# A Perceiver layer on one core: the softmax denominators of its local attention, from key tiles added up on GpSimd

## The chip, the cores and the metric

The kernel runs on one core of a Trainium2 chip. The metric is the device time of one launch in microseconds, as the median of several runs. The engines are TensorE (PE; its weight loads are PEld), VectorE (DVE), ScalarE (ACT), GpSimd (POOL) and SyncE (SP), which here starts the DMAs.

## The reference

A latent x of 512 tokens with 512 channels passes three blocks: cross-attention to 8192 context tokens with an MLP behind it, causal local self-attention, and a gated feed-forward block with FP4 rounding. The change is in the second:

```python
qkv = layernorm(x) @ Wqkv                      # 16 heads of 32 channels
q, k = rope(q), rope(k)
dist = idx[None, :] - idx[:, None]
allowed = (dist <= 0) & (dist >= -255)         # a window of 256 keys
scores = where(allowed, q @ k.T / sqrt(32), -inf)
x = x + (softmax(scores) @ v) @ Wout
```

All of it is in float32; the kernel splits values into float16 halves where it multiplies them in float16.

## The kernel before

The program has four stages, one after the other: projections of the context, cross-attention (the longest), the local attention (names that begin with `local_`), and the feed-forward block (`ffn_`). Each engine has its own instruction list, written out by Python loops, and engines wait for each other by semaphores.

The local stage first makes q, k and v. VectorE, GpSimd and ScalarE apply the rotary embedding there: GpSimd multiplies by the cosines (`t_cos`, L1771), VectorE by the sines (L1859), and VectorE adds both (L1862). The DMA then stacks the float16 halves in `kq_stack`, and later turns the feed-forward weights with transposing DMAs.

Then follow 16 groups, one for each query tile t (128 tokens) and each g of four heads. Query tile 0 sees one key tile, tile 1 two, tiles 2 and 3 three each. The loop on TensorE is a pipeline over rounds n (L2103). In round n it makes:

- `scores_for_maxima(n, u)`: scores of group n with queries on partitions, so that VectorE (`maxima`, L1880) can take row maxima; unit u holds four, two or one heads. The banks of `pre_ps` alternate;
- `row(n - 1)` (L2048): these maxima turned into one row; ScalarE (`set_row`, L1807) copies it into `kq_stack`, where the next product subtracts it;
- `turned_scores(n - 2, i)` (L2062, with the mask L2066): scores with keys on partitions, for key tile i. ScalarE (`exps`, L1815) writes their exponentials to `prT`, a ring of 8 tiles;
- `values(n - 3, step)` (L2083): for each key tile four products with v, and four with a matrix of ones which sum the exponentials over keys, all in float32. The first nk steps are values, the next nk are ones, two steps for each u;
- `back(n - 5)` (L2098): the output projection of a group.

VectorE, in its round n, does `maxima(n, 0)`, then `normalise(n - 4)` (a reciprocal of the denominators L1887, a product L1890), then the other maxima. Behind these stand either `add` (L1895, L1900; rounds 9, 13, 17) or up to three pieces of `first_tile` (L1912 to L1951), which prepares the first tile of the feed-forward block out of the latent: in round 11 L1921 / L1924, L1925 / L1927, L1928, in round 12 L1924, L1925 / L1927, L1928 / L1924, L1925, in round 14 L1927, L1928 / L1930 / L1933, in round 15 L1936, L1937 / L1939, L1940 / L1942, in round 16 L1945 / L1947 / L1949. ScalarE makes the float16 high half of the output (`high_out`, L1820) and GpSimd the low half `o_low` (L1776), its only work in these rounds.

Of the kernel before, what the change touches and what calls it, by code (L numbers as in the profile page):

```python
# [22 lines left out]
ALU = mybir.AluOpType  # L23
# [7 lines left out]
P = 128  # L31
T = 512
D = 512
# [6 lines left out]
HD = D // H  # L40
G = 4
HG = H // G
# [20 lines left out]
TILE_RING = 8  # L63
# [19 lines left out]
class Chain:  # L83
# [14 lines left out]
    def wait(self):  # L98
        self.eng.wait_ge(self.sem, self.n + self.moving)
# [35 lines left out]
def perceiver(nc, a, out):  # L135

    with ExitStack() as whole:
# [1514 lines left out]
        with ExitStack() as st:  # L1652
# [12 lines left out]
            kq_stack = sb("kq_stack", [P, 2, H, T], F16)  # L1665
            v = sb("v_local", [P, TT, D])
            prT = sb("prT", [P, TILE_RING, D])
            top = sb("top", [P, 2, HG], F16)
            inv = sb("inv", [P, 2, P])
            o_norm = sb("o_norm", [P, 2, P])  # L1670
# [10 lines left out]
            turned_out = sem("turned_out_l")  # L1681
            qk_ready = sem("qk_ready")
            qk_out = sem("qk_out")
            rot_ready = sem("rot_ready")
            cos_done = sem("cos_done")
            roped = sem("roped")
            r_high = sem("r_high")
            r_low = sem("r_low")
# [29 lines left out]
            pre_upto = [sum(pre_units[:n + 1]) for n in range(NG)]  # L1718
            tiles_upto = [sum(seen[t][1] for t, _ in groups[:n + 1]) for n in range(NG)]


            pre_turns = []
            for n in range(NG + 1):
# [39 lines left out]
            @block.gpsimd  # L1763
            def _(pool):
                pool.wait_ge(const_in, 64)
                nc.gpsimd.tensor_copy(maskb[:], mask[:]).then_inc(consts, 1)
                nc.gpsimd.tensor_copy(identb[:], ident[:]).then_inc(consts, 1)
                for m in range(2 * G):
                    pool.wait_ge(qk_out, m + 1)
                    wait(pool, roped, m - 1)  # L1770
                    nc.gpsimd.tensor_tensor(t_cos[:, m % 2], qk[:, m % 2], cos[:], ALU.mult).then_inc(cos_done, 1)  # L1771
                for n, (t, g) in enumerate(groups):
                    pool.wait_ge(o_scaled, n + 1)
                    pool.wait_ge(o_high, n + 1)
                    tokens = slice(t * P, (t + 1) * P)
                    nc.gpsimd.tensor_tensor(oT[:, 1, g, tokens], o_norm[:, n % 2], oT[:, 0, g, tokens],  # L1776
                                            ALU.subtract).then_inc(o_low, 1)

            @block.scalar
            def _(act):  # L1780
                layer_norm_scalar(act, var_ready, sd_ready, 2)
                for t in range(TT):
                    act.wait_ge(turned, t + 1)
                    nc.scalar.activation(xnT[:, 0, :, t * P:(t + 1) * P], by_chunk(t), ACT.Copy).then_inc(turned_high, 1)

                def high(m):

                    act.wait_ge(roped, m + 1)
                    nc.scalar.activation(r_hi[:, m // G, m % G], rotated[:, m % 2], ACT.Copy,
                                         scale=(1.0, SCALE)[m // G]).then_inc(r_high, 1)  # L1790

                for m in range(2 * G):
                    if m >= 2:
                        high(m - 2)
                    act.wait_ge(qk_ready, m + 1)
                    wait(act, roped, m - 1)
                    nc.scalar.activation(qk[:, m % 2], s_ps[:, 0, m % 2], ACT.Copy, scale=1.0 / WSCALE).then_inc(qk_out, 1)
                high(2 * G - 2)
                high(2 * G - 1)
                for t in range(TT):  # L1800
                    act.wait_ge(v_ready, t + 1)
                    nc.scalar.activation(v[:, t], t_ps[:, t % 2], ACT.Copy, scale=1.0 / WSCALE).then_inc(v_read, 1)

                def set_row(n):
                    t, g = groups[n]
                    act.wait_ge(row_ready, n + 1)
                    nc.scalar.activation(kq_stack[KROWS:KROWS + 1, 1, g * HG:(g + 1) * HG, t * P:(t + 1) * P],  # L1807
                                         pre_ps[KROWS:KROWS + 1, turn_of[("row", n, 0)] % 2].rearrange("p (j q) -> p j q", j=HG),
                                         ACT.Copy).then_inc(row_set, 1)

                def exps(n, i):
                    c = tiles_upto[n] - seen[groups[n][0]][1] + i
                    act.wait_ge(s_ready, c + 1)
                    wait(act, p_read, c + 1 - TILE_RING)
                    nc.scalar.activation(prT[:, c % TILE_RING], score_ps[:, c % 2], ACT.Exp).then_inc(p_ready, 1)  # L1815

                def high_out(n):
                    t, g = groups[n]
                    act.wait_ge(o_scaled, n + 1)
                    nc.scalar.activation(oT[:, 0, g, t * P:(t + 1) * P], o_norm[:, n % 2], ACT.Copy).then_inc(o_high, 1)  # L1820

                for n in range(NG + 4):
                    tiles = seen[groups[n - 2][0]][1] if 2 <= n < NG + 2 else 0
                    if tiles:
                        exps(n - 2, 0)
                    if 1 <= n <= NG:
                        set_row(n - 1)
                    for i in range(1, tiles):
                        exps(n - 2, i)
                    if n >= 4:  # L1830
                        high_out(n - 4)
                    if n == NG + 3:
                        act.wait_ge(first_turned, 1)
                        nc.scalar.activation(first_T[:, 0], pre_ps[:, 0].rearrange("p (k c) -> p k c", c=P),
                                             ACT.Copy).then_inc(first_high, 1)

            @block.vector
            def _(dve):
# [15 lines left out]

                for m in range(2 * G):

                    dve.wait_ge(rot_ready, m + 1)
                    wait(dve, roped, m - 1)
                    chain.link(nc.vector.tensor_tensor(t_sin[:, m % 2], s_ps[:, 1, m % 2], sin[:], ALU.mult))  # L1859
                    dve.wait_ge(cos_done, m + 1)  # L1860
                    wait(dve, r_low, m - 1)
                    nc.vector.tensor_tensor(rotated[:, m % 2], t_cos[:, m % 2], t_sin[:, m % 2], ALU.add).then_inc(roped, 1)  # L1862
                    if m >= 1:
                        low(m - 1)
# [19 lines left out]

                def normalise(n):
                    dve.wait_ge(p_read, tiles_upto[n])
                    nc.vector.reciprocal(inv[:, n % 2], od_ps[:, n % 2, P:2 * P]).then_inc(inv_ready, 1)  # L1887
                    dve.wait_ge(inv_ready, n + 1)
                    wait(dve, o_low, n - 1)
                    nc.vector.tensor_tensor(o_norm[:, n % 2], od_ps[:, n % 2, 0:P], inv[:, n % 2],  # L1890
                                            ALU.mult).then_inc(o_scaled, 1)
# [91 lines left out]
            def _(pe):  # L1983
# [9 lines left out]
                def rotate(m):  # L1993
                    pe.wait_ge(qk_out, m + 1)
                    wait(pe, roped, m - 1)
                    nc.tensor.matmul(s_ps[:, 1, m % 2], rot[:], qk[:, m % 2], start=True, stop=True).then_inc(rot_ready, 1)

                for m in range(2 * G):
                    wait(pe, qk_out, m - 1)
# [67 lines left out]
                                                    start=False, stop=True)  # L2067
                    last.then_inc(s_ready, 1)

                def values(n, step):  # L2070


                    t, g = groups[n]
                    k0, nk = seen[t]
                    at, i = divmod(step, nk)
                    c = tiles_upto[n] - nk + i
                    if at == 0:
                        pe.wait_ge(p_ready, c + 1)
                    if step == 0:
                        wait(pe, o_scaled, n - 1)  # L2080
                    for j in range(HG):
                        head = g * HG + j
                        last = nc.tensor.matmul(od_ps[j * HD:(j + 1) * HD, n % 2, at * P:(at + 1) * P],  # L2083
                                                ones[:] if at else v[:, k0 + i, head * HD:(head + 1) * HD],
                                                prT[:, c % TILE_RING, j * P:(j + 1) * P], start=i == 0, stop=i == nk - 1)
                    if at:
                        last.then_inc(p_read, 1)

                def back(n):

# [12 lines left out]
                for n in range(NG + 5):  # L2103
# [3 lines left out]
                    for u in range(max(units, scored, weighted, 1)):  # L2107
                        if u < units:
                            scores_for_maxima(n, u)
                        if u < scored:  # L2110
                            turned_scores(n - 2, u)
                        if u < weighted:
                            values(n - 3, 2 * u)
                            values(n - 3, 2 * u + 1)
                        if u == 0 and 1 <= n <= NG:
                            row(n - 1)
                    if n >= 5:
                        back(n - 5)
                    if n == NG + 3:
# [352 lines left out]
```

## Time and profile before

| | |
|---|---|
| median of 3 runs | 1332.82 us (1330.89 to 1335.74) |
| the profiled execution | 1333.27 us |
| its span, first to last instruction | 1331.4 us |
| granted TensorE clock, mean | 0.995 of full speed |
| the 16 groups of local attention | about 1156 to 1229 us of the span |
| TensorE, VectorE, ScalarE, GpSimd busy in 1157.0 to 1229.2 us (72.2 us) | 67.0, 56.3, 36.4, 7.2 us |

A time in a row counts from the start of the span. "Busy" of TensorE includes the pipelined ends of its products, so the distance between two starts says more than the length of one. A bracket at the end of a row is the idle time of the engine just before it and the operation that ended it.

### The profile page before, as it was taken

To read this page: it belongs to the slowest core of one execution; us is meant where nothing else is said; L and a number is where in the kernel's file an instruction comes from. 1 tells how busy PE (TensorE), PEld (TensorE's weight loads), DVE (VectorE), ACT (ScalarE), POOL (GpSimd) and SP (SyncE) were. 2 spreads that over 40 slices of the span, in tenths; PEclk is the share of its full clock that TensorE was granted. 3 is DMA by queue.
4 is the path that set the end of the run, shared out by engine and by line. 5 is a ranking of instruction groups with operands and counts; after the bars stand their busy time and mean duration, and the time that the engine had idled before them with its cause. 6 is when DMAs were issued, how large, how long until landed. Compare 5 with 4: busy or idle time off the path is not lost. (4 is left out here: it accounts for less than half of the span.)

```text
span 1331.4 us, 39304 instructions
## 1 busy us (share of the span) xinstructions
PE 1292.7 (97%) x16386; PEld 673.5 (51%) x16386; DVE 1084.9 (81%) x1791; ACT 989.2 (74%) x2026; POOL 717.5 (54%) x340
## 2 busy tenths in 40 slices
PE   8999999998999999999999999999999999999998
PEld 5444444443455555555555555555554445576454
DVE  6678888886888988888888888888986665588885
ACT  5456654564999999999999999999999832354332
POOL 1322222124788988888898889889887001111121
PEclk9999999999999999999999999999999999999999
DMA  8687886775462122122212221221211040690000
GB/s 274 189 204 220 248 241 183 203 234 152 119 190 77 40 72 69 36 66 68 72 40 71 70 56 55 65 67 37 72 59 31 4 151 1 143 215 2 1 9 25
DMA packets 127799, 137.50 MB, mean 103 GB/s; under 512 B 44995, under 2 KB 108995, under 8 KB 125699
## 3 DMA queue, kind: packets, MB, share of 16 engines
q1 hardware_dynamic: 127622, 134.98, 36.1%
q8 instruction: 130, 2.13, 0.7%
q14 instruction: 47, 0.39, 0.1%
HBM read 75.70 MB, written 44.17 MB: 90 GB/s over the span
## 5 line engine op out<-in xcount | busy, mean ns | idle before, releaser
L1444 DVE TENSOR_REDUCE early<-attend_banks 128x1 f32<-128x512 f32 x952 | 590.0, 682 | 66.1 <-PE attend_banks L1144 64.7
L1602 POOL TENSOR_TENSOR early<-early,attend_prob 128x1152 f32<-128x1152 f32 x210 | 556.6, 2650 | 43.1 <-ACT attend_prob L1401 22.9
L1401 ACT ACTIVATE attend_prob<-attend_banks 128x512 f32<-128x512 f32 x1024 | 555.5, 600 | 20.8 <-PE attend_banks L1184 12.7
L1184 PE MATMUL attend_banks<-early,k_first 97*32 97x512 f16 x2560 | 269.2, 383 | 5.6 <-PEq L303 4.0
L1144 PE MATMUL attend_banks<-k_first,early 96*32 96x512 f16 x2272 | 214.8, 383 | 0.6
L1184 PE MATMUL attend_banks<-early,attend_k_rest 97*32 97x512 f16 x1536 | 160.8, 380 | 1.1 <-ACT attend_prob L1401 0.9
L1357 ACT ACTIVATE attend_banks<-attend_banks,early 128x512 f32<-128x512 f32 x238 | 160.1, 673 | 0.0
L1144 PE MATMUL attend_banks<-attend_k_rest,early 96*32 96x512 f16 x1536 | 142.4, 379 | 0.0
L1197 PE MATMUL attend_banks<-attend_prob,wkv_area 128*32 128x512 f32 x1024 | 136.0, 592 | 0.0
L1197 PE MATMUL attend_banks<-attend_prob,attend_vh_odd 128*32 128x512 f32 x1024 | 135.2, 592 | 0.0
L1144 PEld LDWEIGHTS attend_banks<-k_first,early 96*32 96x32 f16 x2272 | 74.5, 96 | 100.3 <-DVE early L1444 74.5
L532 POOL TENSOR_TENSOR project_w_whole<-project_grid,project_qscale 128x704 f32<-128x704 f32 x24 | 34.8, 1452 | 165.7 <-DVE project_w_out L713 111.4
L1184 PEld LDWEIGHTS attend_banks<-early,k_first 97*32 97x32 f16 x2560 | 84.9, 96 | 51.7 <-ACT attend_prob L1401 35.9
L1208 PE MATMUL attend_banks<-attend_prob,ones 128*32 128x96 f32 x2208 | 96.0, 245 | 0.0
L590 ACT ACTIVATE project_v<-project_v_ps 128x512 f32<-128x512 f32 x64 | 38.0, 599 | 77.8 <-PE project_v_ps L868 77.8
L1208 PEld LDWEIGHTS attend_banks<-attend_prob,ones 128*32 128x32 f32 x2208 | 75.4, 110 | 35.4 <-issue 1.2
L1144 PEld LDWEIGHTS attend_banks<-attend_k_rest,early 96*32 96x32 f16 x1536 | 48.9, 95 | 66.4 <-DVE early L1444 50.3
L521 POOL TENSOR_TENSOR project_qn<-early,project_qinv 128x704 f32<-128x704 f32 x24 | 36.3, 1514 | 71.0 <-issue 42.1
L866 PE MATMUL project_v_ps<-project_w_hi,project_yT_hi 128*128 128x512 f16 x192 | 73.2, 381 | 0.7 <-ACT project_v L590 0.7
L849 PE MATMUL project_k_ps<-project_yT_hi,project_w_hi 128*128 128x512 f16 x192 | 72.5, 379 | 1.0 <-ACT project_yT_hi L556 1.0
L868 PE MATMUL project_v_ps<-project_w_hi,project_yT_lo 128*128 128x512 f16 x192 | 73.0, 380 | 0.0
L867 PE MATMUL project_v_ps<-project_w_lo,project_yT_hi 128*128 128x512 f16 x192 | 73.0, 380 | 0.0
(233 smaller groups left out, 1963.2 us busy)
## 6 DMA issues: line engine op xcount, KB each, us to landing
v_scratch<-project_v SPq DMA_DIRECT2D x16, 1024.0 KB, 8.3
early<-in_ctx_dram SPq DMA_DIRECT2D x16, 768.0 KB, 6.4
k_first<-k_scratch SPq DMA_DIRECT2D x36, 256.0 KB, 3.4
k_scratch<-project_k_hi SPq DMA_DIRECT2D x64, 128.0 KB, 2.9
k_scratch<-project_k_lo SPq DMA_DIRECT2D x64, 128.0 KB, 3.1
attend_vh_odd<-v_scratch SPq DMA_DIRECT2D x8, 1024.0 KB, 5.3
wkv_area<-v_scratch SPq DMA_DIRECT2D x7, 1024.0 KB, 5.1
attend_k_rest<-k_scratch SPq DMA_DIRECT2D x24, 256.0 KB, 3.4
```

The lines of the kernel that those rows point to most:

```text
L849: last = nc.tensor.matmul(k_ps[:, g % 2], (w_lo if p == 2 else w_hi)[:, 0, k, cols], (yT_lo if p == 1 else yT_hi)[:, u, k], start=(k, p) = ...
L866: nc.tensor.matmul(v_ps[:, t % 2], yT_hi[:, u, k, cols], w_hi[:, 1, k], start=k == 0, stop=False)
L867: nc.tensor.matmul(v_ps[:, t % 2], yT_hi[:, u, k, cols], w_lo[:, 1, k], start=False, stop=False)
L868: last = nc.tensor.matmul(v_ps[:, t % 2], yT_lo[:, u, k, cols], w_hi[:, 1, k], start=False, stop=k == CK - 1)
L1144: last = nc.tensor.matmul(pre_ps[c * HD:(c + 1) * HD, bank, :], q_stack[0:KROWS, h, queries], keys_at(s, part * BLK, (part + 1) * BLK)[0:K ...
L1184: last = nc.tensor.matmul(s_ps[c * HD:(c + 1) * HD, s_bank(h, n), :], key_rows[:, c * HD:(c + 1) * HD], q_stack[0:KROWS + 1, h, :], start= ...
L1197: last = nc.tensor.matmul(pv_ps[t * HD:(t + 1) * HD, :], vh[s][:, BT * q + t, :], prob[:, q % PSLOTS, t, :], start=q == 0, stop=q == QUADS ...
L1208: last = nc.tensor.matmul(den_ps[t * HD:(t + 1) * HD, 0:P - HD], ones[:], of_block(prob[:, q % PSLOTS, n, 0:ADDED], t), start=q == 0 and n ...
L1357: nc.scalar.activation(pre_ps[:, bank], pre_ps[:, bank], ACT.Exp, bias=tile_low[:, s, SUM_J, part:part + 1], accum_out=part_sum[:, s, part ...
L1401: nc.scalar.activation(prob[:, q % PSLOTS, t, :], s_ps[:, s_bank(h, BT * q + t)], ACT.Exp).then_inc(p_ready, 1)
L1444: nc.vector.tensor_reduce(tile_low[:, s, j, part:part + 1], pre_ps[:, bank], AX.X, ALU.max, negate=True).then_inc(pre_read, 1)
L1602: nc.gpsimd.tensor_tensor(sums, sums, prob[:, q % PSLOTS, 0:POOL_TILES, 0:ADDED], ALU.add).then_inc(pool_summed, 1)
```

## The change

The exponentials of a group's two or three key tiles are added on GpSimd into `tile_sum` (two buffers), and TensorE makes one set of four ones-products from the sum. This holds for the groups 4 to 14. The groups 0 to 3 have one tile, and the last group keeps its three sets. `values(n, i)` now makes only value products, one key tile for each u; the ones-products stand in `denominators(n)`, behind all units of the round and ahead of `back`. `rot_ready` is renamed `side_ready` and counts the denominators too; `cos_done` is renamed `pool_made` and counts the sums too. GpSimd issues the sums of group n before the low half of group n - 2. An exponential waits for the sum that reads its old tile.

```diff
+            tile_sum = sb("tile_sum", [P, 2, D])
...
+            def summed(n):
+                return seen[groups[n][0]][1] > 1 and n < NG - 1
+            def sums_until(n):
+                return 2 * G + sum(seen[groups[k][0]][1] - 1 for k in range(n + 1) if summed(k))
...
-                for n, (t, g) in enumerate(groups):
-                    pool.wait_ge(o_scaled, n + 1)
-                    pool.wait_ge(o_high, n + 1)
-                    tokens = slice(t * P, (t + 1) * P)
-                    nc.gpsimd.tensor_tensor(oT[:, 1, g, tokens], o_norm[:, n % 2], oT[:, 0, g, tokens],
-                                            ALU.subtract).then_inc(o_low, 1)
+                def sum_tiles(n):
+                    nk = seen[groups[n][0]][1]
+                    c0 = tiles_upto[n] - nk
+                    pool.wait_ge(p_ready, c0 + 2)
+                    pool.wait_ge(side_ready, 2 * G + n - 1)
+                    nc.gpsimd.tensor_tensor(tile_sum[:, n % 2], prT[:, c0 % TILE_RING], prT[:, (c0 + 1) % TILE_RING],
+                                            ALU.add).then_inc(pool_made, 1)
+                    if nk == 3:
+                        pool.wait_ge(p_ready, c0 + 3)
+                        pool.wait_ge(pool_made, sums_until(n) - 1)
+                        nc.gpsimd.tensor_tensor(tile_sum[:, n % 2], tile_sum[:, n % 2], prT[:, (c0 + 2) % TILE_RING],
+                                                ALU.add).then_inc(pool_made, 1)
+
+                for n in range(NG + 2):
+                    if n < NG and summed(n):
+                        sum_tiles(n)
+                    if n >= 2:
+                        t, g = groups[n - 2]
+                        pool.wait_ge(o_scaled, n - 1)
+                        pool.wait_ge(o_high, n - 1)
+                        tokens = slice(t * P, (t + 1) * P)
+                        nc.gpsimd.tensor_tensor(oT[:, 1, g, tokens], o_norm[:, n % 2], oT[:, 0, g, tokens],
+                                                ALU.subtract).then_inc(o_low, 1)
...
 def exps(n, i):
-                    wait(act, p_read, c + 1 - TILE_RING)
+                    if c >= TILE_RING:
+                        act.wait_ge(p_read, c + 1 - TILE_RING)
+                        before = next(k for k in range(NG) if tiles_upto[k] > c - TILE_RING)
+                        if summed(before):
+                            act.wait_ge(pool_made, sums_until(before))
+                        else:
+                            act.wait_ge(side_ready, 2 * G + before + 1)
...
 def normalise(n):
                     dve.wait_ge(p_read, tiles_upto[n])
+                    dve.wait_ge(side_ready, 2 * G + n + 1)
...
-                def values(n, step):
+                def values(n, i):
-                    at, i = divmod(step, nk)
-                    if at == 0:
-                        pe.wait_ge(p_ready, c + 1)
-                    if step == 0:
+                    pe.wait_ge(p_ready, c + 1)
+                    if i == 0:
                         wait(pe, o_scaled, n - 1)
                     for j in range(HG):
                         head = g * HG + j
-                        last = nc.tensor.matmul(od_ps[j * HD:(j + 1) * HD, n % 2, at * P:(at + 1) * P],
-                                                ones[:] if at else v[:, k0 + i, head * HD:(head + 1) * HD],
+                        last = nc.tensor.matmul(od_ps[j * HD:(j + 1) * HD, n % 2, 0:P], v[:, k0 + i, head * HD:(head + 1) * HD],
                                                 prT[:, c % TILE_RING, j * P:(j + 1) * P], start=i == 0, stop=i == nk - 1)
-                    if at:
-                        last.then_inc(p_read, 1)
+                    last.then_inc(p_read, 1)
+
+                def denominators(n):
+                    nk = seen[groups[n][0]][1]
+                    if summed(n):
+                        pe.wait_ge(pool_made, sums_until(n))
+                        tiles = [tile_sum[:, n % 2]]
+                    else:
+                        tiles = [prT[:, (tiles_upto[n] - nk + i) % TILE_RING] for i in range(nk)]
+                    for i, tile in enumerate(tiles):
+                        for j in range(HG):
+                            last = nc.tensor.matmul(od_ps[j * HD:(j + 1) * HD, n % 2, P:2 * P], ones[:],
+                                                    tile[:, j * P:(j + 1) * P], start=i == 0, stop=i == len(tiles) - 1)
+                    last.then_inc(side_ready, 1)
...
                         if u < weighted:
-                            values(n - 3, 2 * u)
-                            values(n - 3, 2 * u + 1)
+                            values(n - 3, u)
                         if u == 0 and 1 <= n <= NG:
                             row(n - 1)
+                    if weighted:
+                        denominators(n - 3)
                     if n >= 5:
                         back(n - 5)
```

## Rows read from the trace of the kernel before

**Rows 1.** The page: the span, and busy time, share and instructions of an engine.

```profile
span 1331.4 us, 39304 instructions
...
PE 1292.7 (97%) x16386; PEld 673.5 (51%) x16386; DVE 1084.9 (81%) x1791; ACT 989.2 (74%) x2026; POOL 717.5 (54%) x340
```

**Rows 2.** Groups by shape, PE, 1156 to 1229.3 us: busy, mean ns, idle before.

```profile
L2083 PE MATMUL local_t_ps<-local_prT,ones 128*32 128x128 f32 x288 | 12.3, 276 | 0.0
```

**Rows 3.** Timeline of PE, one round: start, length, operation, [idle before].

```profile
1199.23 0.22 PE L2066 MATMUL local_sl_ps<-local_identb,local_maskb 128*128 128x128 bf16 x1
1199.38 0.64 PE L2083 MATMUL local_t_ps<-local_prT,local_v_local 128*32 128x128 f32 x16
1199.86 0.39 PE L2048 MATMUL local_sl_ps<-identh,local_top 128*1 128x128 f16 x4
1200.34 0.34 PE L2034 MATMUL local_sl_ps<-local_kq_stack 96*128 96x384 f16 x1
...
1202.36 0.64 PE L2083 MATMUL local_t_ps<-local_prT,ones 128*32 128x128 f32 x16
1202.94 0.34 PE L2034 MATMUL local_sl_ps<-local_kq_stack 96*128 96x384 f16 x1
```

**Rows 4.** Timeline of PE: max(n,1) of rounds 11, 12, 14, 15.

```profile
1189.82 0.34 PE L2034 MATMUL local_sl_ps<-local_kq_stack 96*128 96x384 f16 x1 [0.44 <-DVE local_top L1880]
...
1195.00 0.34 PE L2034 MATMUL local_sl_ps<-local_kq_stack 96*128 96x384 f16 x1
...
1205.83 0.34 PE L2034 MATMUL local_sl_ps<-local_kq_stack 96*128 96x384 f16 x1 [0.25 <-DVE local_top L1880]
...
1211.69 0.34 PE L2034 MATMUL local_sl_ps<-local_kq_stack 96*128 96x384 f16 x1 [0.62 <-DVE local_top L1880]
```

**Rows 5.** Timeline of DVE, rounds 14 to 17.

```profile
1208.92 0.56 DVE L1880 TENSOR_REDUCE local_top<-local_sl_ps 128x1 f16<-128x384 f32 x1 [0.86 <-PE local_sl_ps L2039]
1209.39 0.14 DVE L1927 TENSOR_SCALAR r<-r 128x1 f32<-128x1 f32 x1
...
1215.26 0.17 DVE L1936 TENSOR_SCALAR late<-late 128x32 f32<-128x32 f32 x1
...
1220.47 0.96 DVE L1887 RECIPROCAL local_inv<-local_t_ps 128x128 f32<-128x128 f32 x1
```

**Rows 6.** Timeline of ACT, exponentials of rounds 14 and 16.

```profile
1206.54 0.60 ACT L1815 ACTIVATE local_prT<-local_sl_ps 128x512 f32<-128x512 f32 x1 [0.33 <-PE local_sl_ps L2062]
1207.96 0.60 ACT L1815 ACTIVATE local_prT<-local_sl_ps 128x512 f32<-128x512 f32 x1 [0.83 <-PE local_sl_ps L2066]
...
1217.31 0.60 ACT L1815 ACTIVATE local_prT<-local_sl_ps 128x512 f32<-128x512 f32 x1
```

**Rows 7.** Stretches: length, busy us of each engine.

```profile
1215.00:1225.00 10.00, 10.00 (x198) 6.89 (x197) 9.59 (x19) 4.88 (x10) 1.65 (x4) 1.00 0.01 3
```

**Rows 8.** One line: ns min/median/max.

```profile
L1771 POOL TENSOR_TENSOR turned_area<-turned_area,early x8: 1264/1268/1271, 1118.2 to 1141.5; 128x512 f32<-128x512 f32 x8
```

**Rows 9.** The same for DVE's addition of two SBUF operands.

```profile
L1862 DVE TENSOR_TENSOR turned_area<-turned_area x8: 691/904/906, 1121.8 to 1144.5; 128x512 f32<-128x512 f32 x8
```

**Rows 10.** Timeline of POOL and DVE, ropes of the local stage.

```profile
1124.23 1.27 POOL L1771 TENSOR_TENSOR turned_area<-turned_area,early 128x512 f32<-128x512 f32 x1 [2.18 <-ACT turned_area L1797]
...
1125.14 0.91 DVE L1862 TENSOR_TENSOR turned_area<-turned_area 128x512 f32<-128x512 f32 x1
```

**Rows 11.** Timeline of POOL and DVE, feed-forward stage.

```profile
1279.49 1.15 POOL L2231 TENSOR_TENSOR ffn_hqT<-ffn_whole_T,ffn_hqT 128x512 f16<-128x512 f32 x1 [6.46 <-ACT ffn_whole_T L2259]
1279.85 0.83 DVE L2300 TENSOR_SCALAR ffn_qscale_f<-ffn_amax_f 128x32 f32<-128x32 f32 x1
```

**Rows 12.** Timeline of DVE and POOL, round 16.

```profile
1218.91 0.69 DVE L1947 TENSOR_TENSOR late<-late 128x512 f32<-128x512 f32 x1
...
1219.11 0.78 POOL L1776 TENSOR_TENSOR late<-local_o_norm,late 128x128 f16<-128x128 f32 x1 [3.91 <-ACT late L1820]
```

**Rows 13.** Timeline of POOL, attention stage: two sums in a row.

```profile
487.54 2.65 POOL L1602 TENSOR_TENSOR early<-early,attend_prob 128x1152 f32<-128x1152 f32 x1 [0.24 <-ACT attend_prob L1401]
```

More of the change, by code:

```diff
@@ L1683, in perceiver @@
             qk_out = sem("qk_out")
-            rot_ready = sem("rot_ready")
-            cos_done = sem("cos_done")
+            side_ready = sem("side_ready")
+            pool_made = sem("pool_made")
             roped = sem("roped")
@@ L1770, in _ @@
                     wait(pool, roped, m - 1)
-                    nc.gpsimd.tensor_tensor(t_cos[:, m % 2], qk[:, m % 2], cos[:], ALU.mult).then_inc(cos_done, 1)
-                for n, (t, g) in enumerate(groups):
-                    pool.wait_ge(o_scaled, n + 1)
-                    pool.wait_ge(o_high, n + 1)
-                    tokens = slice(t * P, (t + 1) * P)
-                    nc.gpsimd.tensor_tensor(oT[:, 1, g, tokens], o_norm[:, n % 2], oT[:, 0, g, tokens],
-                                            ALU.subtract).then_inc(o_low, 1)
+                    nc.gpsimd.tensor_tensor(t_cos[:, m % 2], qk[:, m % 2], cos[:], ALU.mult).then_inc(pool_made, 1)
+                def sum_tiles(n):
[20 more added lines that the diff above has]
+                                                ALU.subtract).then_inc(o_low, 1)
             @block.scalar
@@ L1855, in _ @@
                 for m in range(2 * G):
-                    dve.wait_ge(rot_ready, m + 1)
+                    dve.wait_ge(side_ready, m + 1)
                     wait(dve, roped, m - 1)
                     chain.link(nc.vector.tensor_tensor(t_sin[:, m % 2], s_ps[:, 1, m % 2], sin[:], ALU.mult))
-                    dve.wait_ge(cos_done, m + 1)
+                    dve.wait_ge(pool_made, m + 1)
                     wait(dve, r_low, m - 1)
@@ L1995, in rotate @@
                     wait(pe, roped, m - 1)
-                    nc.tensor.matmul(s_ps[:, 1, m % 2], rot[:], qk[:, m % 2], start=True, stop=True).then_inc(rot_ready, 1)
+                    nc.tensor.matmul(s_ps[:, 1, m % 2], rot[:], qk[:, m % 2], start=True, stop=True).then_inc(side_ready, 1)
                 for m in range(2 * G):
```

## The prediction

> **What bounds the kernel now.** I read the page first: TensorE is busy for 97% of 1331.4 us [rows 1]. The groups by line between 1156 and 1229 us, the part of the local stage that the diff touches, come next: 288 records of ones-products, two to a product, so 144 products, 12.3 us busy, with no idle time before them [rows 2]. A mean of 276 ns is pipelined length, not cost; the cost is the pitch, and for that the timeline of one round is needed.
>
> A round n is one pass of the loop at L2103. I call max(n,u) the products of `scores_for_maxima(n, u)`, and S(n) the start of max(n,1), which waits until VectorE has reduced max(n,0), as they share a bank. S is 1189.82, 1195.00, 1200.34, 1205.83, 1211.69 for n = 11 to 15 [rows 3, 4], so the rounds from 11 to 14 last 5.18, 5.34, 5.49 and 5.86. In round 11 TensorE has no wait, in 13 and 14 it waits at the end for `local_top` (0.25, 0.62) [rows 4], and in 12 VectorE is nearly as late.
>
> A round has two halves. From max(n,1) to max(n,3), 1200.34 to 1202.94, TensorE alone sets the pace: 2.60 us [rows 3]. VectorE then idles 0.86 before the last reduction, which starts at S + 3.09, and goes on at S + 3.56 with the steps of `first_tile` [rows 5]. From max(n,3) to S(n+1) TensorE needs 5.18 - 2.60 = 2.58 (round 11), and VectorE needs 0.49 to be released, the reduction, the steps, the next reduction. So in rounds 12 to 14 both halves must be asked separately. After the last reduction (round 15) VectorE is the bound: 9.59 us busy in the 10 us from 1215 to 1225 (third busy figure of the row) [rows 7].
>
> **What is removed on TensorE.** 16 records from 1199.38 to 1199.86 are 0.48 us, 0.03 a record; a set of four products (one key tile) is 8 records, 0.24 us [rows 3]. Entering the f32 products costs 0.09 (1199.23 + the pitch of 0.06 = 1199.29, start 1199.38), leaving them for products with a full weight load costs 0.10 (16 records take 0.58 from 1202.36 to 1202.94) [rows 3]. Groups 4 to 14 are summed. In a round with three key tiles six sets become four: -0.48. The ones now stand by themselves ahead of `back`: one more entry and exit, +0.19. TensorE's round becomes 5.18 - 0.29 = 4.89. The half after max(n,1) loses two sets, -0.48; the half after max(n,3) gains 0.43 and loses the one value set that moves to u = 1, +0.19.
>
> **Where it arrives.** In rounds 3 and 4 the ones move behind `row`, whose result ScalarE turns into the wait of the next scores: about -0.2 each. In rounds 5 and 6 nothing waits and nothing is saved: +0.19 each. Rounds 7 to 9 (two key tiles): -0.24 + 0.19 each. Round 10: VectorE's steps end it, but its middle half is a set shorter, -0.24. Together -0.4. From round 11 on the middle half brings VectorE's last reduction 0.48 forward, which is worth 0.48 wherever VectorE ends the round, and 0.29 where TensorE does.
>
> **What is added on GpSimd.** Up to two additions of 128x512 f32 a round, 1.27 us each by the same shape and operation kind [rows 8]. ScalarE's exponential of tile 1 starts at S + 0.71 and ends at S + 1.31 [rows 4, 6]. That of tile 2, now at S + 2.13 [rows 4, 6], comes 0.24 sooner and ends at S + 2.49. With 0.1 for the release the first addition runs from S + 1.4 to S + 2.67. The second also waits for the first; the gap of such a pair is 0.24 [rows 13], so it runs from S + 2.91 to S + 4.18. Between 0.05 and 0.3 for that gap moves this end by 0.2. TensorE wants the sum at the end of the next round, S(n+1) + 2.4 or so: 3 us spare, no wait. Queued behind the second addition is `o_low` of the group two before, late by at most 1 us at S + 4.7. Its reader `back` stands in the next round, `normalise` in the one after: covered. `o_low` frees o_norm for a normalise two rounds off; covered. The wait of the exponentials on the sum of the tile eight back is for one that ended a round before: nothing, and without that cover it would stop ScalarE by the lateness. The added waits on VectorE (16) and ScalarE find their value there; their own cost is between 0 and 0.03 each (the pitch of VectorE's small steps leaves no more), I take 0. Denominators come later but VectorE's `normalise` stands behind max(n,0), behind them on TensorE: nothing.
>
> **What the additions meet.** This is the largest term. DVE's L1862, two SBUF operands, takes 691 ns with no GpSimd work beside it and 904 with it [rows 9]: at 1125.14 it found L1771 running until 1125.50 and ended at 1126.05, 0.55 after that [rows 10]. It was stopped until GpSimd was done. A `tensor_scalar` of 128x32, SBUF to SBUF, ended at 1280.68, 0.04 after GpSimd's 1280.64, and took 0.83 [rows 11], where my S(15) row of the same shape took 0.17 [rows 5]. It goes the other way too: a 128x128 `o_low`, issued at 1219.11 under L1947, took 0.78 [rows 12], of which 0.49 lay before L1947's end at 1219.60. The reductions, `normalise` and `add` have a PSUM operand or one SBUF operand; only steps of `first_tile` pay. With VectorE's 0.48 gain they now begin at S + 3.08, inside the second addition, which holds them until S + 4.18:
> - round 11: its second step (L1924, two operands) should end at 3.43, ends at 4.20: +0.77. Net -0.48 + 0.77 = +0.29.
> - round 12: the first step is L1924: +0.96, net +0.48.
> - round 13: `add` and bn_stats, not stopped: -0.48 (5.01, above TensorE's 4.89).
> - round 14: the second step, L1928: +0.77, net +0.29.
> - round 15: the first step L1936 (the shape of [rows 11]): 3.25 becomes 4.22, +0.97; less 0.48, +0.49.
> - round 16: exponential 1 of group 14 starts at S(15) + 5.62 [rows 4, 6], about 0.3 sooner after; group 14's additions run at 6.05 to 7.32 and 7.56 to 8.83. VectorE's L1947 comes at about 7.7, would end at 8.4, and ends 0.55 after 8.83: +0.99. VectorE has no room there [rows 5, 7], and `normalise(13)` (1220.47) and all behind it move.
>
> The Trainium skill ("SBUF — State Buffer", section "Who interferes with whom") says that a VectorE instruction with two SBUF inputs, or in a two-port mode, and a reading GpSimd instruction exclude each other, and that whichever issues second blocks fully. The trace agrees with the exclusion, but not to the last 0.14 us: a full 0.69 after 1125.50 would end L1862 at 1126.19, and it ended at 1126.05 [rows 10]. By the rule read so the sum would be 6 x 0.14 = 0.8 us higher than below.
>
> **Sum.** -0.4 + 0.29 + 0.48 - 0.48 + 0.29 + 0.49 + 0.99 = +1.7 us. The profiled execution took 1333.27 us, with 1.9 around its span; the median shown is 1332.82. On the median this gives 1334.5.
>
> **Rivals.**
> 1. The stops don't fall there (the additions start 1 us earlier or later than worked out, or VectorE's steps slip between them). Then only TensorE and VectorE count: -0.4, round 11 -0.29, round 12 -0.45 (TensorE's 4.89 bounds), 13, 14 and 15 -0.48 each: -2.6, or 1330.2. For it: two of the six hits are single steps of 0.15 us. Against: the window is 1.27 us wide and begins before the steps do.
> 2. Slower: the stops multiply. GpSimd's `o_low` follows at once and takes the operands again before VectorE's next step; 0.3 in rounds 11, 12 and 15 (0.9), full restarts (6 x 0.14), and the one-element steps of round 10 stopped as well (0.6; no row shows that shape beside GpSimd): 1.7 + 2.3 = +4.0, or 1336.8. It decides when GpSimd's next start beats VectorE's next issue, some 0.1 us apart by my times.
> 3. Slower: GpSimd's sums come late and TensorE waits at `denominators`. It needs 3 us of lateness; in round 17 only 0.3 is spare, but there VectorE is the bound. If every round of three tiles paid 1 us: +7, 1340.
>
> **How the numbers follow.** The forecast gets 0.62, rival 1 0.22, rival 2 0.11, rival 3 0.03, anything else 0.02. No case but the third leaves 0.3% (4.0 us, about what this kernel's measurement can tell) far behind. The forecast's own range is -0.5 (gaps of 0.05, one hit less) to +3 (two `o_low` stops): 1332.3 to 1335.8. With the bounds of the first two rivals, and both signs: 1330.0 to 1337.0. Faster by over 0.3% 0.04, slower 0.09 (half of rival 2, rival 3, a little more), within 0.87.
>
> **What would show it.** After: 144 instead of 288 records of ones at L2083's successor (36 sets become 18), in one block ahead of L2098's; rounds of about 4.9 to 5.8; VectorE's idle before its last reduction 0.4 instead of 0.86; the first two-operand step after it near 1.0 us long instead of 0.16 in rounds 11, 12 and 14; L1947's successor above 1.5 us. It is wrong if those steps keep 0.16 us (rival 1), if TensorE shows waits for tile_sum (rival 3), or if steps without two SBUF operands stretch.

## The result, and the profile after

The changed kernel took 1336.27 us, median of 20 runs (1332.79 to 1338.58), against 1333.14 for 20 runs of the kernel before: a ratio of 1.0021, with a 95% interval of 1.0014 to 1.0028, some 2.8 us slower. In a second comparison the ratio was 1.0016 (1.0002 to 1.0029). The forecast was 1.7 us slower, in a range of 1330.0 to 1337.0.

The page of the changed kernel, span and busy time:

```profile
span 1331.7 us, 39066 instructions
...
PE 1289.8 (97%) x16242; PEld 669.2 (50%) x16242; DVE 1092.6 (82%) x1791; ACT 990.1 (74%) x2026; POOL 740.5 (56%) x358
```

TensorE's busy time fell by 2.9 us against [rows 1] and the span did not. The spans of two profiled executions don't settle a matter of 2 us, though: in the profile before, the clock granted to TensorE was halved for a stretch at the start of the feed-forward stage, in the one after it was not. The windows from 1242 to 1250 us show it (the third number from the end is the granted clock, the kernel before first), and so do the chains of work that ended last (start, length, operation; again before, then after).

```profile
1242.00:1250.00 8.00, 6.89 (x35) 4.33 (x36) 7.62 (x15) 2.72 (x6) 1.16 (x1) 0.79 0.01 2
```

```profile
1242.00:1250.00 8.00, 5.33 (x35) 3.57 (x36) 7.69 (x14) 2.63 (x5) 1.16 (x1) 1.00 0.01 2
```

```profile
1243.11 1.12 PE ffn_w_ps L2398 x4
1244.22 2.93 PE ffn_g_ps L2412 x12
```

```profile
1244.67 0.66 PE ffn_w_ps L2441 x4
1245.33 1.95 PE ffn_g_ps L2455 x12
```

The same 16 instructions took 4.05 us before and 2.61 after. In both chains VectorE's rounding steps stand ahead of them. The halved clock is the lower of the engine's two levels, 1.2 against 2.4 GHz. Over the launches of the repeat below the mean granted clock was 0.995 for both kernels, so I don't put these 1.4 us down to the change, and from here on the stage of the groups is measured by itself: from VectorE's first reduction of maxima to the first instruction of the feed-forward stage, L262. Before (timeline of VectorE):

```profile
1157.23 1.29 DVE L1880 TENSOR_REDUCE local_top<-local_sl_ps 128x4 f16<-128x512 f32 x2 [5.99 <-PE local_sl_ps L2039]
...
1229.24 0.69 DVE L262 BATCH_NORM_STATS2 stats<-x 128x6 f32<-128x512 f32 x1 [0.62 <-PEq L1652]
```

The same engine in the changed kernel, with the rows that answer to [rows 5] between (L1912 are the reductions, L1954 to L1982 the steps of `first_tile`):

```profile
1156.88 1.29 DVE L1912 TENSOR_REDUCE local_top<-local_sl_ps 128x4 f16<-128x512 f32 x2 [6.02 <-PE local_sl_ps L2072]
...
1191.94 0.56 DVE L1912 TENSOR_REDUCE local_top<-local_sl_ps 128x1 f16<-128x384 f32 x1 [0.59 <-PE local_sl_ps L2072]
...
1192.60 0.77 DVE L1957 TENSOR_TENSOR r<-r 128x1 f32<-128x1 f32 x1
1193.40 0.35 DVE L1958 TENSOR_TENSOR r<-r,ve 128x1 f32<-128x1 f32 x1
...
1197.91 0.95 DVE L1957 TENSOR_TENSOR r<-r 128x1 f32<-128x1 f32 x1
...
1208.86 0.14 DVE L1960 TENSOR_SCALAR r<-r 128x1 f32<-128x1 f32 x1
1209.04 0.77 DVE L1961 TENSOR_TENSOR r<-r 128x1 f32<-128x1 f32 x1
...
1214.97 0.97 DVE L1969 TENSOR_SCALAR late<-late 128x32 f32<-128x32 f32 x1
...
1219.57 1.65 DVE L1980 TENSOR_TENSOR late<-late 128x512 f32<-128x512 f32 x1
...
1230.81 0.69 DVE L262 BATCH_NORM_STATS2 stats<-x 128x6 f32<-128x512 f32 x1 [0.62 <-PEq L1652]
```

The stage lasts 1230.81 - 1156.88 = 73.93 us after, and 1229.24 - 1157.23 = 72.01 before: +1.92 us. That lies at the lower edge of the interval of the runs. The second profile of the changed kernel gave 73.93 again. What stopped VectorE is in the timeline of GpSimd (L1786 is the first addition, L1791 the second, L1802 the low half):

```profile
1190.67 1.27 POOL L1786 TENSOR_TENSOR local_tile_sum<-local_prT 128x512 f32<-128x512 f32 x1 [1.67 <-ACT local_prT L1847]
1192.09 1.27 POOL L1791 TENSOR_TENSOR local_tile_sum<-local_tile_sum,local_prT 128x512 f32<-128x512 f32 x1
1193.31 0.43 POOL L1802 TENSOR_TENSOR late<-local_o_norm,late 128x128 f16<-128x128 f32 x1
...
1208.53 1.27 POOL L1791 TENSOR_TENSOR local_tile_sum<-local_tile_sum,local_prT 128x512 f32<-128x512 f32 x1
...
1214.64 1.27 POOL L1791 TENSOR_TENSOR local_tile_sum<-local_tile_sum,local_prT 128x512 f32<-128x512 f32 x1
...
1219.39 1.28 POOL L1791 TENSOR_TENSOR local_tile_sum<-local_tile_sum,local_prT 128x512 f32<-128x512 f32 x1
```

L1957, a product of one element in each partition with both operands in the on-chip memory, was issued at 1192.60, 0.51 after the second addition, and took 0.77 us instead of 0.16; it ended at 1193.37, the addition at 1193.36. The next, L1958, met the low half and took 0.35 instead of 0.16. L1969, issued at 1214.97, took 0.97 instead of 0.17 and ended 0.03 after the addition of 1214.64. L1980, issued under the addition of 1219.39, took 1.65 instead of 0.69, until 0.55 after that addition's end. The one-element `tensor_scalar` of 1208.86 ran under the addition of 1208.53 in 0.14 and was not stopped.

TensorE's groups by shape, which answer to [rows 2], and its timeline (L2067 starts a unit of maxima; S(n) is the start of max(n,1), as in the prediction, and the rows of 1189.29, 1194.78, 1200.68, 1205.73, 1211.84 are S(11) to S(15)):

```profile
L2127 PE MATMUL local_t_ps<-local_tile_sum,ones 128*32 128x128 f32 x88 | 4.6, 281 | 0.0
...
L2127 PE MATMUL local_t_ps<-local_prT,ones 128*32 128x128 f32 x56 | 2.7, 279 | 0.0
```

```profile
1189.29 0.34 PE L2067 MATMUL local_sl_ps<-local_kq_stack 96*128 96x384 f16 x1 [0.19 <-DVE local_top L1912]
...
1191.83 0.42 PE L2127 MATMUL local_t_ps<-local_tile_sum,ones 128*32 128x128 f32 x8
1192.19 0.82 PE L2140 MATMUL local_ol_ps<-early,late 128*128 128x512 f16 x3
...
1194.78 0.34 PE L2067 MATMUL local_sl_ps<-local_kq_stack 96*128 96x384 f16 x1 [0.45 <-DVE local_top L1912]
...
1200.68 0.34 PE L2067 MATMUL local_sl_ps<-local_kq_stack 96*128 96x384 f16 x1 [0.84 <-DVE local_top L1912]
...
1205.73 0.34 PE L2067 MATMUL local_sl_ps<-local_kq_stack 96*128 96x384 f16 x1
...
1211.84 0.34 PE L2067 MATMUL local_sl_ps<-local_kq_stack 96*128 96x384 f16 x1 [1.06 <-DVE local_top L1912]
```

The ones-products are 88 + 56 = 144 records. Rounds 11 to 14 last 5.49, 5.90, 5.05 and 6.11 us, where [rows 3, 4] give 5.18, 5.34, 5.49 and 5.86; the idle times in brackets name VectorE's reduction, which stands behind the stopped steps.

### The profile page after: what moved, and what is told of

Its sections match the earlier page's. It is cut to its first block and busy times, and to the rows that moved or that the text cites. A ratio compares the mean times of both kernels' runs of the same rounds, so it can differ in the third digit from the quotient of the medians.

```text
span 1331.7 us, 39066 instructions
## 1 busy us (share of the span) xinstructions
PE 1289.8 (97%) x16242; PEld 669.2 (50%) x16242; DVE 1092.6 (82%) x1791; ACT 990.1 (74%) x2026; POOL 740.5 (56%) x358
```

## The experiments

All were timed against the kernel before on the same chip. "Stage" is the length defined above, from each run's profile; it was 72.01 us before and 73.93 changed.

**The changed kernel again** (no edit).

> The changed kernel itself, again, beside the others on one chip. Both theories: ratio to the kernel before near the measured 1.002 (+2 to +3.5 us). The stage of the 16 groups ends 1.9 us later relative to its start, as in its first profile, if that profile is typical.

Measured: ratio 1.0016 (1.0002 to 1.0029), stage 73.93. The loss is there again, and the stage repeats to the hundredth.

**TensorE's part alone.** The additions are left out, and with them ScalarE's and TensorE's waits for them, so the denominators are of one key tile only.

```diff
-                        pe.wait_ge(pool_made, sums_until(n))
-                        tiles = [tile_sum[:, n % 2]]
+                        tiles = [prT[:, (tiles_upto[n] - 1) % TILE_RING]]
...
-                    if n < NG and summed(n):
-                        sum_tiles(n)
```

> GpSimd adds nothing; the ones-products of groups 4 to 14 read the last key tile alone, so the denominators leave out the other tiles. TensorE's, ScalarE's and VectorE's instructions stay those of the changed kernel. Theory (GpSimd's additions stop VectorE's steps): the stops of 0.6 to 1.1 us in rounds 11, 12, 14, 15, 16 go and the saving of TensorE shows: 2.6 us faster than before, ratio 0.998; rounds 11 to 14 last 4.9, 4.9, 5.0, 5.4 us. Rival (the ones-products in a block of their own, behind the units, are what costs): not faster than before, rounds as in the changed kernel (5.5, 5.9, 5.05, 6.1).

Measured: ratio 0.9987 (0.9978 to 0.9997), stage 69.93. Timeline of VectorE, first and last row of the stage and the two steps that had been stopped (L1952 is the changed kernel's L1957):

```profile
1156.41 1.29 DVE L1907 TENSOR_REDUCE local_top<-local_sl_ps 128x4 f16<-128x512 f32 x2 [5.98 <-PE local_sl_ps L2067]
...
1192.13 0.16 DVE L1952 TENSOR_TENSOR r<-r 128x1 f32<-128x1 f32 x1
...
1196.92 0.17 DVE L1952 TENSOR_TENSOR r<-r 128x1 f32<-128x1 f32 x1
...
1226.34 0.69 DVE L262 BATCH_NORM_STATS2 stats<-x 128x6 f32<-128x512 f32 x1 [0.62 <-PEq L1652]
```

The steps take 0.16 us again and rounds 11 to 14 last 4.98, 4.99, 5.06 and 5.42. TensorE's rearrangement is worth 2.08 us; so GpSimd's additions, in the changed kernel, cost 4.00. The rival, that the block of ones-products is the cost, falls. The gain was 0.5 short of what I expected: see the next section.

**GpSimd's part alone.** The kernel before, its TensorE untouched, with the additions put in and read by nobody. The low half stands behind them as in the changed kernel, and the exponentials wait for the sum that reads their old tile.

```diff
+                for n in range(NG + 2):
+                    if n < NG and summed(n):
+                        sum_tiles(n)
```

> The kernel before, with the changed kernel's additions on GpSimd put in and read by nobody; TensorE unchanged. Theory: the additions alone cost, though less in each round than in the changed kernel, as VectorE's steps begin 0.48 us later after max(n,1): 0.43 in round 11, 0.62 in round 12, 0.24 in round 14, 0.44 in round 15, 0.67 and 0.85 on the steps of round 16, together +3.2 us, ratio 1.0024. Rival (TensorE's new order is the cost): 0, ratio 1.000.

Measured: ratio 1.0019 (1.0010 to 1.0028), stage 74.73, +2.72 us where I expected +3.2. Timeline of VectorE (L1954 and L1977 are the changed kernel's L1957 and L1980):

```profile
1157.89 1.29 DVE L1910 TENSOR_REDUCE local_top<-local_sl_ps 128x4 f16<-128x512 f32 x2 [6.08 <-PE local_sl_ps L2069]
...
1199.56 0.53 DVE L1954 TENSOR_TENSOR r<-r 128x1 f32<-128x1 f32 x1
...
1221.37 1.65 DVE L1977 TENSOR_TENSOR late<-late 128x512 f32<-128x512 f32 x1
...
1232.62 0.69 DVE L262 BATCH_NORM_STATS2 stats<-x 128x6 f32<-128x512 f32 x1 [0.62 <-PEq L1652]
```

Rounds 11 to 14 last 5.51, 5.89, 5.49 and 6.12. Three of them are those of the changed kernel to 0.02 us, although TensorE does two sets more. In these rounds the second addition starts 2.8 us after S(n) in both kernels (here 1198.81 in round 12, whose S is 1196.00), and VectorE goes on when it ends: TensorE's saving is not seen in the length of such a round at all. Only in round 13, with no step that can be stopped, does it appear (5.49 here, 5.05 with TensorE's change). That is why the additions cost 2.72 beside the old TensorE and 4.00 beside the new one. Most of the miss of 0.5 lies behind S(15), where the additions cost 1.57 (19.12 us to the end of the stage, 17.55 before) and I had worked out 1.96.

**One addition.** GpSimd adds tiles 0 and 1, TensorE makes a second set from tile 2.

```diff
-                    if nk == 3:
-                        pool.wait_ge(p_ready, c0 + 3)
-                        pool.wait_ge(pool_made, sums_until(n) - 1)
-                        nc.gpsimd.tensor_tensor(tile_sum[:, n % 2], tile_sum[:, n % 2], prT[:, (c0 + 2) % TILE_RING],
-                                                ALU.add).then_inc(pool_made, 1)
...
-                        tiles = [tile_sum[:, n % 2]]
+                        tiles = [tile_sum[:, n % 2]] + [prT[:, (tiles_upto[n] - 1) % TILE_RING]] * (nk == 3)
```

> The changed kernel with only the first addition on GpSimd (tiles 0 and 1); TensorE makes a second set of ones-products from tile 2. Theory (the second addition is what stops VectorE's steps): steps keep 0.16 us, TensorE's rounds are a set (0.24) longer than without it: rounds 11 to 14 at 5.2, 5.2, 5.2, 5.4; the stage of the groups lasts 70.9 us (72.0 before, 73.9 changed), 1.1 us faster than before, ratio 0.9992. Rival (any addition on GpSimd slows VectorE in the round): rounds of 5.4 and more, slower than before.

Measured: ratio 0.9997 (0.9989 to 1.0006), no difference that can be told; stage 71.47. I expected 70.9. Rounds 11 to 14 last 5.20, 5.20, 5.21 and 5.42: no step is stopped, and in the first three TensorE has no wait for VectorE at S(n+1) (0.15 us of it in the fourth). I had missed round 16, where the one addition of group 14 still stands beside the steps. Timeline of VectorE (L1957 here is the product in round 14, L1976 the two-operand step in round 16), then of GpSimd:

```profile
1206.86 0.16 DVE L1957 TENSOR_TENSOR r<-r 128x1 f32<-128x1 f32 x1
...
1215.76 1.65 DVE L1976 TENSOR_TENSOR late<-late 128x512 f32<-128x512 f32 x1
```

```profile
1215.33 1.53 POOL L1786 TENSOR_TENSOR local_tile_sum<-local_prT 128x512 f32<-128x512 f32 x1 [3.08 <-ACT local_prT L1843]
```

The addition of 1215.33 itself took 1.53 us instead of 1.27; a `tensor_scalar` of 512 elements on VectorE had begun 0.02 before it. The two-operand step then ended 0.55 after the addition.

**Groups 13 and 14 not summed.** One constant: `n < NG - 1` becomes `n < NG - 3` in `summed`.

> The changed kernel with groups 13 and 14 not summed, so that GpSimd has no addition beside the steps of rounds 15 and 16. Theory: rounds 11 to 14 as in the changed kernel (5.5, 5.9, 5.06, 6.1), the two stops behind them (0.97, about 1.1) gone, 0.5 lost as TensorE has its old sets at the end: stage 72.6 us, 0.6 us slower than before, ratio 1.0005. Rival (the loss lies in rounds 11 to 14 alone): stage 73.9.

Measured: ratio 1.0002 (0.9992 to 1.0012), stage 72.59. Rounds 11 to 14 keep their stops (5.49, 5.89, 5.06, 6.10) and 1.34 us are saved behind them, although TensorE has its old sets there: of the 1.92 us that the stage lost, more than half lay behind S(15).

**GpSimd only writes.** The kernel without sums, with fills of an unused tile where the additions stood (denominators again of one tile).

```diff
-                    nc.gpsimd.tensor_tensor(tile_sum[:, n % 2], prT[:, c0 % TILE_RING], prT[:, (c0 + 1) % TILE_RING],
-                                            ALU.add).then_inc(pool_made, 1)
+                    nc.gpsimd.memset(filled[:], 0.0).then_inc(pool_made, 1)
```

> The kernel without sums (the ones-products of groups 4 to 14 read the last key tile alone, so the denominators leave out the other tiles), and in the additions' places GpSimd fills an unused 128x1280 f32 tile, which writes the on-chip memory and reads nothing, 1.1 to 1.3 us each, at the additions' times. Theory (the operand reads of both engines exclude each other): VectorE's two-operand steps keep 0.16 us in rounds 11, 12, 14 and 0.69 in round 16; a one-operand tensor_scalar of 128x32 or 128x512 may still be stopped; rounds 5.0, 5.0, 5.06, 5.4, stage 70 to 71. Rival (GpSimd's being busy is what stops VectorE, whatever it does): 5.5, 5.9, 5.06, 6.1, stage 73.9.

Measured: ratio 0.9986 (0.9977 to 0.9995), stage 70.80; rounds 4.98, 5.11, 5.06 and 5.46. Timeline of VectorE, then of GpSimd (L1789 and L1793 are the fills, L1803 the low half):

```profile
1198.60 0.15 DVE L1955 TENSOR_TENSOR r<-r 128x1 f32<-128x1 f32 x1
...
1198.98 0.15 DVE L1958 TENSOR_SCALAR r<-r 128x1 f32<-128x1 f32 x1
...
1199.36 0.38 DVE L1955 TENSOR_TENSOR r<-r 128x1 f32<-128x1 f32 x1
...
1214.23 0.72 DVE L1967 TENSOR_SCALAR late<-late 128x32 f32<-128x32 f32 x1
```

```profile
1198.17 1.16 POOL L1793 MEMSET local_filled<- 128x1280 f32 x1
1199.30 0.43 POOL L1803 TENSOR_TENSOR late<-local_o_norm,late 128x128 f16<-128x128 f32 x1
...
1213.75 1.17 POOL L1793 MEMSET local_filled<- 128x1280 f32 x1
```

The two-operand product of 1198.60 runs under the fill that began at 1198.17 in its usual 0.15 us. The same line at 1199.36 meets the low half, which reads, and takes 0.38. The `tensor_scalar` at 1214.23 has one operand and is stopped by the fill: 0.72, until 1214.95, 0.03 after the fill's end. The one-element `tensor_scalar` of 1198.98 is not. So it is no general slowness beside a busy GpSimd: the two-operand steps were stopped by instructions that read, the `tensor_scalar` of 128x32 also by one that only writes. The stage is 0.87 us longer than that of the kernel without sums, 0.70 of it behind S(15), where this stop is. The Trainium skill ("SBUF — State Buffer", section "Who interferes with whom") states the same split: an instruction with two SBUF inputs contends with a GpSimd instruction that reads, not with one that only writes. For a two-port mode, which a `tensor_scalar` can enter, it says that it contends with GpSimd and makes no such exception. The trace agrees with the first (0.15 beside the fill, 0.38 beside the low half); it fits the second (0.72), but no row shows the mode.

**The second addition late.** It waits until VectorE has taken the first maxima of the next round, which stand behind the steps; the low half follows it, a round later than in the changed kernel; groups 13 and 14 are not summed.

```diff
+                def second(n):
+                    c0 = tiles_upto[n] - seen[groups[n][0]][1]
+                    pool.wait_ge(p_ready, c0 + 3)
+                    pool.wait_ge(pool_made, sums_until(n) - 1)
+                    pool.wait_ge(pre_read, pre_upto[n + 2] + 1)
+                    nc.gpsimd.tensor_tensor(tile_sum[:, n % 2], tile_sum[:, n % 2], prT[:, (c0 + 2) % TILE_RING],
+                                            ALU.add).then_inc(pool_made, 1)
...
+                for n in range(NG + 3):
+                    if 1 <= n <= NG and summed(n - 1) and seen[groups[n - 1][0]][1] == 3:
+                        second(n - 1)
+                    if n >= 3:
+                        t, g = groups[n - 3]
...
                     if n < NG and summed(n):
                         sum_tiles(n)
```

> The changed kernel with the second addition of a group held back on GpSimd until VectorE has taken the first maxima of the next round, that is behind the steps of first_tile, the low half moved behind it, and groups 13 and 14 no longer summed (they keep their three sets on TensorE). Theory: no step of rounds 11, 12, 14, 15, 16 is stopped, TensorE finds each sum in time: 2.4 us faster than before, ratio 0.9982. Rival (GpSimd's work beside VectorE costs wherever it stands, or the late sums make TensorE wait): 0 to +3 us, with idle time of TensorE ahead of tile_sum's products.

Measured: ratio 0.9985 (0.9973 to 0.9997), stage 70.50. Timeline of GpSimd (L1786 first, L1794 second addition), then of VectorE (L1969 is the product of round 11):

```profile
1193.93 1.27 POOL L1786 TENSOR_TENSOR local_tile_sum<-local_prT 128x512 f32<-128x512 f32 x1
1197.03 1.28 POOL L1794 TENSOR_TENSOR local_tile_sum<-local_tile_sum,local_prT 128x512 f32<-128x512 f32 x1 [1.83 <-DVE local_top L1924]
```

```profile
1195.52 0.16 DVE L1969 TENSOR_TENSOR r<-r 128x1 f32<-128x1 f32 x1
```

GpSimd does the same kind of work between 1193.93 and 1198.31, leaves the gap from 1195.20 to 1197.03, and the steps from 1195.33 to 1196.25 fall into it. Rounds 11 to 14: 4.98, 4.99, 5.05, 5.43, those of the kernel without sums. TensorE has no idle time ahead of `tile_sum`: the sum ready at 1198.31 is used at 1199.73. Leaving out groups 13 and 14 alone gave 72.59, so the move in time (of the second addition and the low half) is worth 2.09 us.

**The same, with the ones-products placed by round.**

```diff
                         if u < weighted:
                             values(n - 3, u)
+                            if u == weighted - 1 and (5 <= n <= 9 or n >= NG):
+                                denominators(n - 3)
...
-                    if weighted:
+                    if weighted and not (5 <= n <= 9 or n >= NG):
                         denominators(n - 3)
```

> The version with the late second addition, and the ones-products put behind the last value set in rounds 5 to 9 and from 16 on, at the round's end in the others. Theory: where TensorE bounds the round (5 to 9) the block's own entry and exit (0.21) go, about 1.3 us over them, and 0.4 in the tail; rounds 10 to 15 stay as in the late version (4.98, 4.98, 5.06, 5.43): stage 68.8 us, 3.2 us faster than before, ratio 0.9976. Rival (VectorE's reductions bound those rounds too): stage 70.5, ratio 0.9989, with idle time of TensorE behind VectorE in rounds 7 to 9.

Measured: ratio 0.9984 (0.9974 to 0.9995), 1331.34 against 1333.31 us. Stage, from VectorE's first reduction to L262:

```profile
1159.40 1.29 DVE L1924 TENSOR_REDUCE local_top<-local_sl_ps 128x4 f16<-128x512 f32 x2 [5.98 <-PE local_sl_ps L2084]
...
1228.69 0.69 DVE L262 BATCH_NORM_STATS2 stats<-x 128x6 f32<-128x512 f32 x1 [0.62 <-PEq L1652]
```

69.29 us, 2.72 less than before and 1.2 less than the version above. I expected 68.8. The ratio can't be told from that one's, but both are faster than the kernel before. The early rounds gave what was expected (S(10) comes 1.2 us sooner after the stage's start than in the version above). The tail did not: from S(15) on both last the same, so placing the block does nothing there.

## Why the prediction came out as it did

The step "what the additions meet" was right in its mechanism, places and sizes. By rounds, forecast and measured: round 11 +0.29 and +0.31; round 12 +0.48 and +0.56; round 13 -0.48 and -0.44; round 14 +0.29 and +0.25; round 15 and the tail +1.48 and +1.42. The second addition began 2.80 us after S(11) and ended at 4.07, against 2.91 and 4.18 in the prediction. The 0.24 taken there for the gap between two sums is a misreading of [rows 13]: that idle time was ended by ScalarE, not by the first sum, and the gap measured is 0.15 (1191.94 to 1192.09). It did no harm, as VectorE's steps fell into the addition all the same. L1980 of round 16 took 1.65 us as expected ("above 1.5").

The term that was mis-sized is that of the rounds up to S(11): -0.4 forecast, -0.18 measured. Up to S(8) the change gained 0.19, where the forecast's terms give 0.07; rounds 8 and 9, which I had at -0.05 each, came out longer (4.15 for 4.04 us, 4.39 for 4.27); round 10 gained 0.22 of 0.24. So the miss of 0.2 is a larger one, partly cancelled. Two things stand behind it. A block of one set costs TensorE 0.36 us from its start to the next products (1191.83 to 1192.19), and 0.09 to enter; I had taken 0.24 + 0.10 and 0.09. With four blocks of one set in place of three blocks of two, 0.02 a block makes TensorE's round 4.98 and not 4.89. In rounds 8 and 9 that explains some 0.05 of the 0.16 by which each missed. Another 0.08 in round 8 is a wait that I had put at nothing: TensorE now reaches max(8,3) sooner, and starts it at 1177.54, 0.06 after the end of VectorE's reduction (1176.93 + 0.55), so that the two units are 0.37 apart instead of 0.29.

The kernel without sums fell 0.5 short of its -2.6 for the same reasons: 0.2 in the early rounds, 0.1 each in rounds 11 and 12, the rest in small parts behind them.

Rival 1 (no stops) is excluded by the rows; as a kernel of its own it exists in the version without sums, at -2.1. Rival 2's mechanism is real and small: the low half stopped a following step in rounds 11 and 12 by 0.19 each. Its one-element steps of round 10 are not stopped: round 10 became shorter, 4.79 for 5.01. Rival 3 did not occur: no wait of TensorE for a sum. The Trainium skill ("SBUF — State Buffer", section "Who interferes with whom") says that the second to issue blocks fully. The full restart that the prediction read out of it as an alternative (the stopped instruction begins anew, its whole length behind the block) does not happen: L1957, 0.16 long alone, ends 0.01 after the addition, and L1980, 0.69 long alone, 0.55 after it. The prediction prices that restart for six stops; its own list has five.

Two of its signs were off, though the terms behind them held. It named rounds of 4.9 to 5.8, while its own terms put round 14 at 6.15 (measured 6.11), and an idle time of VectorE before its last reduction of 0.4, where the rows show 0.59.

What stays open: the runs put the loss at 1.9 to 3.7 us, the stage accounts for 1.92. The rest, if there is any, was not found. In the two profiles the time ahead of the stage is 0.35 us shorter in the changed kernel, and the time behind it 1.27 shorter, of which the halved clock is 1.44: nothing there is as large as the stage's own loss.

## What to carry to other kernels

An idle engine is free only where its instructions hold up nobody else's. Before putting elementwise additions on GpSimd, list what VectorE executes in the same microseconds, and look for instructions with two operands in the on-chip memory, and for a `tensor_scalar` of many elements from that memory to itself. A step of one element can lose nearly as much as a large one (0.79 us in round 12, 0.96 for the 512 elements of L1980), because it waits for the end of the other engine's instruction. And if the collision can't be avoided by shape, move it in time: one more wait on GpSimd, whose sum had been ready 4 us before its use (1193.36 and 1197.33), and two groups fewer to add up turned 0.2% slower into 0.15% faster.

## What was not expected of the hardware

GpSimd's reading and its writing don't stop the same instructions. A fill on GpSimd left two-operand products on VectorE alone (0.15 us) and stopped a `tensor_scalar` of 128x32 (0.72 instead of 0.17), while an addition stopped both, and a `tensor_scalar` of one element was stopped by neither (0.14 under an addition, 0.15 under a fill). A stopped two-operand step doesn't start anew when the other engine is done: it ends 0.01 us later if it has one element, and 0.55 later if it has 512 (0.69 alone). A round with a stopped step takes the same time whatever TensorE saves in it (5.49 and 5.51, 5.90 and 5.89, 6.11 and 6.12).
